# Batch norm's statistics from PSUM, one joined product, an early table load and a changed order of small work in a fused conv/attention kernel

## The chip, the core and the metric

The kernel runs on one core of a Trainium2 chip. A core has TensorE (PE in the profile, with its weight loads as PEld), VectorE (DVE), ScalarE (ACT), GpSimd (POOL) and a SyncE (SP) that here only issues DMAs. All of them run their own list of instructions and meet by semaphores. The metric is the device time of one execution in microseconds (us); the kernel before takes 408.95 us, the median of 3 runs between 408.8 and 410.1.

## What is computed

Six layers follow one another on 8 images of 64 channels by 16x16. The change lies in the first two. The other four are an attention with 8 heads, a mixture of 8 experts, a wavelet attention and a mixture of 16 experts, each behind a layer norm over tokens. Layers one and two of the reference, with what matters:

```python
def _L0_conv_ref(x, Wg, bg, Wt, bt, Wp, bp, Ww, bw, gamma, beta):
    g_x = _maxpool2(_conv1x1(x, Wg, bg))          # pooled values
    theta_x = _conv1x1(x, Wt, bt)                 # queries
    phi_x = _maxpool2(_conv1x1(x, Wp, bp))        # pooled keys
    f_div_C = jax.nn.softmax(jnp.einsum('bni,bim->bnm', theta_x, phi_x), axis=-1)
    y = jnp.einsum('bnm,bmi->bni', f_div_C, g_x)
    w_y = _conv1x1(y, Ww, bw)
    mu = w_y.mean(axis=(0, 2, 3)); var = w_y.var(axis=(0, 2, 3))
    w_y = (w_y - mu) * jax.lax.rsqrt(var + EPS) * gamma + beta
    return w_y + x

def _L1_conv_ref(x, w3, w1, ...):                 # signs of values, signs of weights
    out1 = bn(conv(binary_act(x + b11), bin_weight(w3), pad=1), g1, be1, m1, v1)
    out1 = prelu(x + out1 + b12, a1) + b13
    out2 = bn(conv(binary_act(out1 + b21), bin_weight(w1), pad=0), g2, be2, m2, v2) + out1
    return prelu(out2 + b22, a2) + b23
```

## The kernel before

Each engine's list is written out by hand in one function (`block.tensor`, `block.vector`, `block.scalar` and so on). An engine runs its list in order, so an instruction that waits for a semaphore also holds back everything behind it on that engine. On VectorE the helper `step` makes each small instruction wait for the one before it.

The data of the first two layers lie as 128 partitions (two images by 64 channels) by 1024 columns, worked on in two halves of 512 columns. A half fills one bank of PSUM. The path of layer one is this: TensorE projects the images (L1110); VectorE pools two of the four results and ScalarE adds a bias to the other two, which gives `theta` (L655); TensorE makes the products f (L1118) and a small product for the output weights (L1126). VectorE and ScalarE do the softmax (L1390 to L1405). TensorE meanwhile folds attention weights of layer three (L1132), which needs five loaded weights (`attn_loaded`), and only then transposes the softmax (L1141) and makes w_y (L1148) in banks 4 and 5. ScalarE moves w_y to `wy` with its bias (L678), and VectorE takes the statistics from there (L1416, L1417). Each channel lies on two partitions, so the halves of mean and variance are joined by a product with a constant matrix: first the mean (L1154), then the variance (L1157). ScalarE takes the root of three variances (L682) behind a load of its function table, VectorE makes scale and shift of them, scales both halves and adds the input (L1434, L1435).

Layer two: ScalarE takes the signs (L685), TensorE convolves them in nine products a half (L1169), behind a second fold (L1161). VectorE has ten small instructions for the constants of both norms (L1439 to L1443), a split of folded weights (L1447) and two shifts (L1465) to do before it takes the convolution up (L1456). Then, for each half, VectorE adds (L1456), ScalarE takes the positive part (`positive`, L696), VectorE puts the two together (L1458, L1460), ScalarE takes the second signs (L701) and a shifted copy (L703), TensorE does the second convolution (L1177), and VectorE and ScalarE repeat the step into `x2`. The rest of the kernel (layer norm, attention, experts) follows. The helper `keep_clock` issues products whose result nobody reads; before the change it is called once, far behind.

## Time and profile before

| | us |
|---|---|
| median of 3 runs | 408.95 |
| profiled execution, its own time | 408.8 |
| its span, first to last instruction | 407.0 |
| TensorE busy | 346.5 |
| VectorE busy | 283.3 |
| ScalarE busy | 214.6 |
| GpSimd busy | 174.7 |

The span is what the trace covers; 1.8 us of the execution's own time lie around it. Times in the rows below are us from the span's start. The mean granted clock of TensorE over the span is 0.916 of full speed; it takes two levels only, 1.00 (2.4 GHz) and 0.50 (1.2 GHz). The stretch that the change touches runs from 0 to about 46 us. The idle time in brackets at the end of a row says how long the engine stood still before it and what ended that.

### The profile page before, as it was taken

How to read it: one execution, taken by the hardware profiler on the slowest of the kernel's cores; microseconds unless marked ns; L12 is line 12 of the kernel's file. 1: busy time of each engine (PE TensorE's matmuls, PEld its weight loads, DVE VectorE, ACT ScalarE, POOL GpSimd, SP SyncE). 2: the span in 40 equal slices, each digit the busy share in tenths (PEclk: the TensorE clock that was granted, in tenths of full speed). 3: DMA queues.
4: the chain of work that ended last, by engine and by line, in shares of the span. 5: the costliest groups of instructions: out<-in, count | busy, mean ns of one | idle time of the engine just before them, and what ended most of it. 6: DMA issues, size and time to landing. Idle time of an engine off the chain costs nothing.

```text
span 407.0 us, 6942 instructions
## 1 busy us (share of the span) xinstructions
PE 346.5 (85%) x2177; PEld 244.5 (60%) x2179; DVE 283.3 (70%) x679; ACT 214.6 (53%) x527; POOL 174.7 (43%) x178
## 2 busy tenths in 40 slices
PE   5666368999999999999879799857267999999996
PEld 2552256788788878887567344444065766666662
DVE  2867787788877888787579696687796544555541
ACT  0534357777677767778546544360334534444441
POOL 4020125545455554545410000140110599999984
PEclk9967579999999999999988899988568899999999
DMA  6916000000000000000000794000000866666521
GB/s 184 235 30 209 0 0 2 1 2 3 0 0 0 0 0 0 0 0 2 0 2 3 270 404 159 0 0 2 0 1 13 299 219 208 209 210 217 195 101 52
DMA packets 17002, 32.87 MB, mean 81 GB/s; under 512 B 6032, under 2 KB 9808, under 8 KB 16976
## 3 DMA queue, kind: packets, MB, share of 16 engines
q1 hardware_dynamic: 16976, 32.55, 24.2%
q8 instruction: 13, 0.21, 0.2%
q14 instruction: 13, 0.11, 0.1%
HBM read 31.83 MB, written 0.72 MB: 80 GB/s over the span
## 4 chain that ended last, share of the span: by engine, by line
PE 66%; DVE 18%; ACT 7%; issue 4%; DMA 2%; POOL 0%; SPq 0%; DVEq 0%; ACTq 0%; POOLq 0%
PE ps L1019 15%; PE ps L1027 7%; PE ps L853 7%; PE ps L880 7%; PE ps L864 6%; PE ps L975 4%; ACT va_vb L615 2%; PE ps L967 2%; DVE ln L1501 2%; PE ps L829 2%; DVE negmax L1581 2%; DVE XS L379 2%; PE ps L830 2%; PE ps L906 1%; PE ps L1110 1%
## 5 line engine op out<-in xcount | busy, mean ns | idle before, releaser
L502 POOL TENSOR_TENSOR va_vb<-va_vb,rowinv 128x512 f32<-128x512 f32 x64 | 67.1, 1049 | 72.4 <-DVE rowinv L1588 72.4
L615 ACT ACTIVATE va_vb<-ps,negmax 128x256 f32<-128x256 f32 x128 | 59.4, 471 | 11.9 <-DVE negmax L1581 11.7
L1019 PE MATMUL ps<-XS,w3hl 128*128 128x512 f32 x256 | 64.7, 412 | 0.7 <-ACT gT L586 0.7
L730 ACT ACTIVATE wy<-ps 128x512 f32<-128x512 f32 x64 | 38.2, 598 | 47.3 <-PE ps L1019 47.3
L1019 PEld LDWEIGHTS ps<-XS,w3hl 128*128 128x128 f32 x256 | 49.6, 196 | 17.5 <-issue 4.9
L1581 DVE TENSOR_REDUCE negmax<-ps 128x2 f32<-128x512 f32 x64 | 44.0, 687 | 6.4 <-PE ps L853 4.7
L853 PE MATMUL ps<-keys_gates,xcur 128*128 128x256 f32 x256 | 46.5, 303 | 2.2 <-DVE keys_gates L1573 1.4
L864 PE MATMUL ps<-consts,va_vb 128*128 128x128 f32 x256 | 39.4, 277 | 5.1 <-POOL va_vb L502 3.1
L460 POOL TENSOR_TENSOR xn<-T,lnc 128x512 f32<-128x512 f32 x4 | 4.2, 1041 | 92.0 <-DVE lnc L1509 92.0
L853 PEld LDWEIGHTS ps<-keys_gates,xcur 128*128 128x128 f32 x256 | 34.3, 189 | 14.3 <-issue 11.3
L864 PEld LDWEIGHTS ps<-consts,va_vb 128*128 128x128 f32 x256 | 29.7, 147 | 10.5 <-POOL va_vb L502 4.2
L880 PE MATMUL ps<-pT,vproj 128*64 128x256 f32 x256 | 34.5, 392 | 0.0
L606 ACT ACTIVATE keys_gates<-ps 128x512 fp32r<-128x512 f32 x32 | 19.1, 598 | 25.2 <-PE ps L830 25.2
L615 ACT ACTIVATION_READ_ACCUMULATOR va_vb<-ps,negmax 128x1 f32 x128 | 25.7, 201 | 0.0
L599 DVE COPY pT<-ps 128x512 f32<-128x512 f32 x32 | 21.8, 680 | 1.9 <-PE ps L864 1.9
L1573 DVE TENSOR_TENSOR keys_gates<-ps,keys_gates 128x512 fp32r<-128x512 f32 x32 | 21.8, 682 | 1.6 <-ACT keys_gates L606 1.6
L1674 DVE TENSOR_TENSOR theta_qk<-ps,wy 128x512 f32<-128x512 f32 x16 | 11.1, 691 | 15.3 <-ACT wy L730 15.3
L880 PEld LDWEIGHTS ps<-pT,vproj 128*64 128x64 f32 x256 | 15.6, 136 | 8.9 <-issue 1.4
L597 ACT ACTIVATE pT<-ps 128x512 f32<-128x512 f32 x32 | 19.2, 600 | 0.2 <-PE ps L864 0.2
L1588 DVE RECIPROCAL rowinv<-rowsum 128x2 f32<-128x2 f32 x64 | 10.5, 165 | 11.8 <-ACT va_vb L615 9.6
L967 PE MATMUL ps<-XS,w2hl 128*128 128x512 f32 x64 | 17.9, 430 | 0.5 <-ACT x L722 0.5
L829 PE MATMUL ps<-xcur,AH 128*128 128x256 f32 x64 | 17.1, 288 | 0.1
(321 smaller groups left out, 706.4 us busy)
## 6 DMA issues: line engine op xcount, KB each, us to landing
pT<-gates_row SPq DMA_DIRECT2D x18, 512.0 KB, 4.7
vproj<-gates_row SPq DMA_DIRECT2D x16, 512.0 KB, 5.4
gate_row_keys<-gates_row SPq DMA_DIRECT2D x14, 512.0 KB, 5.2
early<-in_f_in SPq DMA_DIRECT2D x1, 2048.0 KB, 9.1
consts<-in_consts SPq DMA_DIRECT2D x1, 816.0 KB, 5.1
x<-in_x SPq DMA_DIRECT2D x1, 512.0 KB, 3.5
w2raw<-in_f_in SPq DMA_DIRECT2D x1, 512.0 KB, 3.6
out<-in_f_out SPq DMA_DIRECT2D x1, 512.0 KB
```

Source lines behind the costliest of these rows:

```text
L502: gp.tensor_tensor(prob[:, n % 4], prob[:, n % 4], rowinv[:, n % 4, :].unsqueeze(2).broadcast_to([P, U, N]), ALU.mult).then_inc(S("p_scale ...
L599: eng.tensor_copy(dst, src).then_inc(S("pT_odd"), 1)
L615: ins = act.activation(prob[:, n % 4, u, :], ps[:, 1 + n % 2, u * N:(u + 1) * N], ACT.Exp, bias=negmax[:, n % 4, u:u + 1], accum_out=rowsu ...
L730: act.activation(act_out[:, kk % 2, :], ps[:, 2 * (kk % 3), :], ACT.Silu).then_inc(S("f3_act"), 1)
L829: pe.matmul(o, AH[:, head].rearrange("p d c -> p (d c)"), xcur[:, g, :], start=True, stop=False)
L853: mm = pe.matmul(ps[:, 1 + n % 2, u * N:(u + 1) * N], xcur[:, g, u * P:(u + 1) * P], K[:, k % 2, n % 2, :], start=(part == 0), stop=(part ...
L864: mm = pe.transpose(ps[:, 3 + n % 2, su * N + u * P:su * N + (u + 1) * P], prob[:, n % 4, u, su * P:(su + 1) * P], ident)
L880: mm = pe.matmul(ps[h * C:(h + 1) * C, 5, 0:N], vproj[:, g, su, head * C:(head + 1) * C], pT[:, (2 * k + h) % 4, su, :], start=(k % 4 == 0 ...
L967: mm = pe.matmul(ps[:, kk % 4, :], w2hl[:, s, e], XS[:, c * CHUNK:(c + 1) * CHUNK], start=(s == 0), stop=(s == 1))
L1019: mm = pe.matmul(ps[:, 2 * (kk % 3) + w, :], w3hl[:, s, e, w * HID:(w + 1) * HID], XS[:, c * CHUNK:(c + 1) * CHUNK], start=(s == 0), stop= ...
L1027: pe.matmul(ps[half, bank, :], out3[:, e, :], hid[kk % RING], start=False, stop=False, skip_group_check=True).then_inc(S("f3_out_chunk"), 1)
L1581: dve.tensor_reduce(negmax[:, n % 4, :], ps[:, 1 + n % 2, :].rearrange("p (u n) -> p u n", u=U), AX.X, ALU.max, negate=True).then_inc(S("m ...
```

## The change

On ScalarE the table of the exponential is asked for as the first instruction of the kernel. Each half of w_y is counted by VectorE out of PSUM, without the bias, as soon as it is there (`wy_ready`), and ScalarE moves it to `wy` only after that (`wy_counted`). Half means and half variances are joined in one product of two columns; the mean's bias is added afterwards. ScalarE scales the second half (`va_act`) while VectorE scales the first. Sums over weights, two small additions and a sum of squares move to later places on VectorE. In front of the join TensorE runs 5 products of `keep_clock`, and 8 more behind the second fold; they multiply constants of the first convolution. The second signs, shifts and positive parts of layer two are issued in another order on ScalarE.

```diff
--- before.py
+++ after.py
@@ -648,6 +648,7 @@
 
         @block.scalar
         def _(act):
+            act.preload_act_table(ACT.Exp)
             act.wait_ge(S("vec_loaded"), 16)
 
             for p in range(2):
@@ -674,12 +675,15 @@
             act.wait_ge(S("f_transposed"), 1)
             act.activation(probT[:, 0:512], ps[:, 0, :], ACT.Copy).then_inc(S("probT_act"), 1)
             for p in range(2):
-                act.wait_ge(S("wy_ready"), p + 1)
+                act.wait_ge(S("wy_counted"), p + 1)
                 act.activation(wy[:, p * 512:(p + 1) * 512], ps[:, 4 + p, :], ACT.Identity,
                                bias=v_("bw")).then_inc(S("wy_evac"), 1)
 
             act.wait_ge(S("bn_var_ready"), 1)
             act.activation(col[:, 11:14], col[:, 8:11], ACT.Sqrt).then_inc(S("bn_std_ready"), 1)
+            act.wait_ge(S("bn_scale_ready"), 1)
+            act.activation(va[:, 512:1024], wy[:, 512:1024], ACT.Identity, scale=col[:, 28:29],
+                           bias=col[:, 29:30]).then_inc(S("va_act"), 1)
             for p in range(2):
                 act.wait_ge(S("x1_ready"), p + 1)
                 act.activation(sgn[:, 2 * p:2 * p + 2, 1:1 + IMG, 1:1 + IMG],
@@ -695,15 +699,23 @@
                 act.wait_ge(S("prelu_in"), so_far + p + 1)
                 act.activation(vb[:, s], va[:, s], ACT.Relu).then_inc(S("positive_ready"), 1)
 
-            for p in range(2):
-                positive(p, 0)
+            def second_signs(p):
                 act.wait_ge(S("r1_ready"), p + 1)
                 act.activation(sgn2[:, p * 512:(p + 1) * 512], r1[:, p * 512:(p + 1) * 512],
                                ACT.Sign, bias=v_("b21")).then_inc(S("sgn2_ready"), 1)
+
+            def shifted(p):
                 act.activation(va[:, p * 512:(p + 1) * 512], r1[:, p * 512:(p + 1) * 512],
                                ACT.Identity, bias=col[:, 37:38]).then_inc(S("r1_shifted"), 1)
-            for p in range(2):
-                positive(p, 2)
+
+            positive(0, 0)
+            second_signs(0)
+            positive(1, 0)
+            shifted(0)
+            second_signs(1)
+            positive(0, 2)
+            shifted(1)
+            positive(1, 2)
             for half in range(2):
                 act.wait_ge(S("x2_transposed"), half + 1)
                 act.activation(T[:, 8 * half:8 * half + 8, :].rearrange("p t c -> p (t c)"), ps[:, 4 + half, :],
@@ -781,7 +793,7 @@
         def keep_clock(pe, bank, products):
 
             for _ in range(products):
-                pe.matmul(ps[:, bank, :], w3s[:, 0, :], sgn2[:, 0:512], start=True, stop=True)
+                pe.matmul(ps[:, bank, :], w3s[:, 0, :], w3s[:, 4:8, :].rearrange("p k m -> p (k m)"), start=True, stop=True)
 
         def ln_pe(pe, n):
 
@@ -1150,19 +1162,18 @@
                 if j % 2 == 1:
                     mm.then_inc(S("wy_ready"), 1)
 
-            pe.wait_ge(S("bn_mean_half"), 1)
-            pe.matmul(ps[:, 6, 0:1], con("halfavg"), col[:, 0:1], start=True,
-                      stop=True).then_inc(S("bn_mu_done"), 1)
-            pe.wait_ge(S("bn_var_half"), 1)
-            pe.matmul(ps[:, 6, 1:2], con("halfavg"), col[:, 4:5], start=True,
-                      stop=True).then_inc(S("bn_var_done"), 1)
+            pe.wait_ge(S("wsign_ready"), 4)
+            keep_clock(pe, 2, 5)
+            pe.wait_ge(S("bn_halves"), 1)
+            pe.matmul(ps[:, 6, 0:2], con("halfavg"), col[:, 0:2], start=True,
+                      stop=True).then_inc(S("bn_joined"), 1)
 
             for h in range(HEADS):
                 mm = pe.matmul(ps[:, 3, h * C:(h + 1) * C], wvT[:, h, :], wu[:, h, :],
                                start=True, stop=True)
             mm.then_inc(S("folded"), 1)
 
-            pe.wait_ge(S("wsign_ready"), 4)
+            keep_clock(pe, 2, 8)
             for p in range(2):
                 pe.wait_ge(S("sgn_ready"), p + 1)
                 for k in range(9):
@@ -1369,20 +1380,6 @@
             ts(pg[:], pooled[:].unsqueeze(2).broadcast_to([P, J, 2, POOLED]), v_("bpg"), None,
                ALU.add).then_inc(S("pg_ready"), 1)
 
-            dve.wait_ge(S("l1_loaded"), 64)
-            ones = [("w3n", w3n, 9 * C, 20), ("w1n", w1n, C, 21)]
-            for _, w, n, c in ones:
-                step(dve.tensor_reduce(col[:, c:c + 1], w[:], AX.X, ALU.add, apply_absolute_value=True))
-
-            step(ts(col[:, 22:23], col[:, 20:21], 1.0 / (9 * C), None, ALU.mult))
-            step(ts(col[:, 23:24], col[:, 21:22], 1.0 / C, None, ALU.mult))
-            step(ts(col[:, 9:10], v_("v1"), EPS_BN, None, ALU.add))
-            step(ts(col[:, 10:11], v_("v2"), EPS_BN, None, ALU.add))
-
-            dve.wait_ge(S("ns_loaded"), 80)
-            step(dve.tensor_tensor_reduce(nsY[:, 0, :], nsA[:], nsA[:], 1.0, 0.0, ALU.mult, ALU.add, nsc[:, 0:1]))
-            dve.nop().then_inc(S("ns_sq_ready"), 1)
-
             f = ps[:, 5:7, :].rearrange("p a (t c) -> p (a t) c", c=POOLED)
             halves = [slice(8 * half, 8 * half + 8) for half in range(2)]
             for half, q in enumerate(halves):
@@ -1403,6 +1400,13 @@
             step(dve.reciprocal(f_col[:, 2, :], f_col[:, 1, :]))
             for q in halves:
                 tt(f_prob[:, q], f_exp[:, q], wide(f_col[:, 2, q], t=8), ALU.mult).then_inc(S("f_prob_ready"), 1)
+            dve.wait_ge(S("l1_loaded"), 64)
+            ones = [("w3n", w3n, 9 * C, 20), ("w1n", w1n, C, 21)]
+            for _, w, n, c in ones:
+                step(dve.tensor_reduce(col[:, c:c + 1], w[:], AX.X, ALU.add, apply_absolute_value=True))
+
+            step(ts(col[:, 22:23], col[:, 20:21], 1.0 / (9 * C), None, ALU.mult))
+            step(ts(col[:, 23:24], col[:, 21:22], 1.0 / C, None, ALU.mult))
             dve.wait_ge(S("f_transposed"), 2)
             dve.tensor_copy(probT[:, 512:1024], ps[:, 1, :]).then_inc(S("probT_vec"), 1)
 
@@ -1411,27 +1415,38 @@
                 stt(AL[:, :, d, :], ps[:, 7, :].rearrange("p (h c) -> p h c", c=C), 1.0 / math.sqrt(C),
                     AH[:, :, d, :].bitcast(F32), ALU.mult, ALU.subtract).then_inc(S("fold_split"), 1)
 
-            dve.wait_ge(S("wy_evac"), 2)
             for p in range(2):
-                step(dve.bn_stats(bn6[:, p, :], wy[:, p * 512:(p + 1) * 512]))
-            dve.bn_aggr(col[:, 0:2], bn6[:].rearrange("p a s -> p (a s)")).then_inc(S("bn_mean_half"), 1)
-            dve.wait_ge(S("bn_mean_half"), 1)
-            dve.wait_ge(S("bn_mu_done"), 1)
-            step(dve.tensor_copy(col[:, 2:3], ps[:, 6, 0:1]))
-            step(tt(col[:, 3:4], col[:, 0:1], col[:, 2:3], ALU.subtract))
-            stt(col[:, 4:5], col[:, 3:4], col[:, 3:4], col[:, 1:2], ALU.mult, ALU.add).then_inc(S("bn_var_half"), 1)
-            dve.wait_ge(S("bn_var_done"), 1)
-            ts(col[:, 8:9], ps[:, 6, 1:2], EPS_BN, None, ALU.add).then_inc(S("bn_var_ready"), 1)
+                dve.wait_ge(S("wy_ready"), p + 1)
+                dve.bn_stats(bn6[:, p, :], ps[:, 4 + p, :]).then_inc(S("wy_counted"), 1)
+            dve.wait_ge(S("wy_counted"), 2)
+            dve.bn_aggr(col[:, 0:2], bn6[:].rearrange("p a s -> p (a s)")).then_inc(S("bn_halves"), 1)
+            step(ts(col[:, 9:10], v_("v1"), EPS_BN, None, ALU.add))
+            step(ts(col[:, 10:11], v_("v2"), EPS_BN, None, ALU.add))
+
+            dve.wait_ge(S("ns_loaded"), 80)
+            step(dve.tensor_tensor_reduce(nsY[:, 0, :], nsA[:], nsA[:], 1.0, 0.0, ALU.mult, ALU.add, nsc[:, 0:1]))
+            dve.nop().then_inc(S("ns_sq_ready"), 1)
+            dve.wait_ge(S("bn_halves"), 1)
+            dve.wait_ge(S("bn_joined"), 1)
+            step(tt(col[:, 3:4], col[:, 0:1], ps[:, 6, 0:1], ALU.subtract))
+            step(stt(col[:, 4:5], col[:, 3:4], col[:, 3:4], ps[:, 6, 1:2], ALU.mult, ALU.add))
+            ts(col[:, 8:9], col[:, 4:5], EPS_BN, None, ALU.add).then_inc(S("bn_var_ready"), 1)
+            step(tt(col[:, 2:3], ps[:, 6, 0:1], v_("bw"), ALU.add))
             dve.wait_ge(S("bn_std_ready"), 1)
             step(dve.reciprocal(col[:, 24:27], col[:, 11:14]))
 
             step(tt(col[:, 28:29], col[:, 24:25], v_("gamma"), ALU.mult))
             step(tt(col[:, 30:31], col[:, 28:29], col[:, 2:3], ALU.mult))
-            step(tt(col[:, 29:30], v_("beta"), col[:, 30:31], ALU.subtract))
+            tt(col[:, 29:30], v_("beta"), col[:, 30:31], ALU.subtract).then_inc(S("bn_scale_ready"), 1)
+            dve.wait_ge(S("bn_scale_ready"), 1)
+            dve.wait_ge(S("wy_evac"), 2)
             dve.wait_ge(S("l0_loaded"), 32)
             for p in range(2):
                 s = slice(p * 512, (p + 1) * 512)
-                step(ts(va[:, s], wy[:, s], col[:, 28:29], col[:, 29:30], ALU.mult, ALU.add))
+                if p == 0:
+                    step(ts(va[:, s], wy[:, s], col[:, 28:29], col[:, 29:30], ALU.mult, ALU.add))
+                else:
+                    dve.wait_ge(S("va_act"), 1)
                 tt(x1[:, s], va[:, s], x0[:, s], ALU.add).then_inc(S("x1_ready"), 1)
 
             for k, (g_, be, m_, b_) in enumerate((("g1", "be1", "m1", "b12"), ("g2", "be2", "m2", "b22"))):
```

VectorE around the statistics, before: bn is the table of statistics, col the columns of small constants.

```order
L1411 SCALAR_TENSOR_TENSOR AL<-ps,AH 128x8x64 [waits fold_high]
L1411 SCALAR_TENSOR_TENSOR AL<-ps,AH 128x8x64
L1416 BN_STATS bn<-wy 128x6 [waits wy_evac]
L1416 BN_STATS bn<-wy 128x6 [waits dve_step]
L1417 BN_AGGR col<-bn 128x2 [waits dve_step]
L1420 COPY col<-ps 128x1 [waits bn_mu_done,bn_mean_half]
L1421 TENSOR_TENSOR col<-col 128x1 [waits dve_step]
L1422 SCALAR_TENSOR_TENSOR col<-col 128x1 [waits dve_step]
L1424 TENSOR_SCALAR col<-ps 128x1 [waits bn_var_done]
L1426 RECIPROCAL col<-col 128x3 [waits bn_std_ready]
```

The same place on VectorE after the change:

```order
L1415 SCALAR_TENSOR_TENSOR AL<-ps,AH 128x8x64
L1420 BN_STATS bn<-ps 128x6 [waits wy_ready] x2
L1422 BN_AGGR col<-bn 128x2 [waits wy_counted]
L1423 TENSOR_SCALAR col<-vec 128x1
L1424 TENSOR_SCALAR col<-vec 128x1 [waits dve_step]
L1427 ISA nsY,nsc<-nsA 128x64 [waits ns_loaded,dve_step]
L1427 ISA nsc 128x1
L1431 TENSOR_TENSOR col<-col,ps 128x1 [waits dve_step,bn_joined,bn_halves]
L1432 SCALAR_TENSOR_TENSOR col<-col,ps 128x1 [waits dve_step]
L1433 TENSOR_SCALAR col<-col 128x1 [waits dve_step]
L1434 TENSOR_TENSOR col<-ps,vec 128x1
L1436 RECIPROCAL col<-col 128x3 [waits bn_std_ready,dve_step]
```

The statistics read PSUM and wait for the product itself, the second round through TensorE is gone, and four small instructions stand between the sums and the join.

TensorE from w_y to the first convolution, after the change (L796 is `keep_clock`, L1172 the second fold, L1180 the convolution):

```order
L1160 MATMUL ps<-probT_rot,early 128x256
L796 MATMUL ps<-w3s 128x512 [waits wsign_ready]
L796 MATMUL ps<-w3s 128x512 x4
L1168 MATMUL ps<-col,consts 128x2 [waits bn_halves]
L1172 MATMUL ps<-early 128x64 x8
L796 MATMUL ps<-w3s 128x512 x8
L1180 MATMUL ps<-sgn,w3s 128x512 [waits sgn_ready]
```

Before, the list read L1148, L1154, L1157, L1161, L1169: 13 products are new between w_y and the convolution.

ScalarE in layer two, before (r1 is layer two's first result, va_vb the input of the positive part):

```order
L696 ACTIVATE va_vb<-va_vb 128x512
L701 ACTIVATE sgn2<-r1,vec 128x512
L703 ACTIVATE va_vb<-r1,col 128x512
L696 ACTIVATE va_vb<-va_vb 128x512
L701 ACTIVATE sgn2<-r1,vec 128x512
L703 ACTIVATE va_vb<-r1,col 128x512
L696 ACTIVATE va_vb<-va_vb 128x512 x2
```

And after:

```order
L700 ACTIVATE va_vb<-va_vb 128x512 [waits prelu_in]
L704 ACTIVATE sgn2<-r1,vec 128x512 [waits r1_ready]
L700 ACTIVATE va_vb<-va_vb 128x512 [waits prelu_in]
L708 ACTIVATE va_vb<-r1,col 128x512
L704 ACTIVATE sgn2<-r1,vec 128x512 [waits r1_ready]
L700 ACTIVATE va_vb<-va_vb 128x512 [waits prelu_in]
L708 ACTIVATE va_vb<-r1,col 128x512
L700 ACTIVATE va_vb<-va_vb 128x512 [waits prelu_in]
```

Each shifted copy (L708) now stands behind the next positive part (L700) instead of ahead of it.

## Rows read from the trace of the kernel before

**Rows 1.** Chain of waits, 9 to 50 us: start, us, engine, line.

```profile
9.47 0.83 ACT L655
10.30 0.46 issue
...
20.86 2.53 PE ps L1148 x8
...
25.59 0.22 DVE col L1417
...
25.85 0.60 PE ps L1154 x2
...
27.79 3.60 PE ps L1161 x16
31.39 3.97 PE ps L1169 x9
```

**Rows 2.** Busy time by stretch: length, engines' busy us, PEclk, DMA share, GB/s.

```profile
14.50:16.68 2.18, 0.01 (x1) 0.00 (x1) 2.12 (x5) 1.22 (x2) 0.00 (x0) 1.00 0.75 109
16.68:18.60 1.92, 1.92 (x16) 1.86 (x16) 1.85 (x4) 0.00 (x0) 0.00 (x0) 1.00 0.98 277
18.90:22.00 3.10, 3.08 (x11) 2.63 (x12) 1.58 (x3) 1.50 (x3) 2.42 (x2) 0.50 1.24 225
22.10:25.40 3.30, 1.27 (x6) 0.77 (x5) 1.92 (x4) 2.66 (x3) 0.88 (x1) 1.00 0.00 0
25.80:35.60 9.80, 8.98 (x31) 5.98 (x32) 6.86 (x26) 2.14 (x4) 0.00 (x0) 0.50 0.30 96
35.80:42.40 6.60, 2.73 (x13) 1.29 (x12) 4.70 (x8) 4.34 (x7) 0.00 (x0) 1.00 0.52 168
42.90:56.00 13.10, 6.41 (x26) 4.67 (x27) 10.92 (x40) 5.57 (x9) 3.53 (x3) 0.50 0.00 0
```

**Rows 3.** Timeline of TensorE, 10 to 32 us: start, us, instruction, idle before.

```profile
16.68 2.00 PE L1132 MATMUL ps<-early 64*128 64x64 f32 x16 [2.17 <-DMA bu<-in_bu]
18.92 1.94 PE L1141 MATMUL ps<-consts,f_prob 128*128 128x128 f32 x8 [0.24 <-DVE f_prob L1405]
```

**Rows 4.** Instruction groups, 9 to 52 us: reductions from PSUM and from SBUF.

```profile
L1390 DVE TENSOR_REDUCE f_col<-ps 128x8 f32<-128x512 f32 x2 | 1.4, 691 | 0.5 <-PE ps L1118 0.5
...
L1401 DVE TENSOR_REDUCE f_col<-f_both 128x8 f32<-128x512 f32 x2 | 1.3, 680 | 0.0
```

**Rows 5.** Timeline of VectorE, 18 to 46 us.

```profile
21.50 1.28 DVE L1411 SCALAR_TENSOR_TENSOR AL<-ps,AH 128x512 fp32r<-128x512 f32 x2
24.13 1.42 DVE L1416 BATCH_NORM_STATS2 bn<-wy 128x6 f32<-128x512 f32 x2 [1.35 <-ACT wy L678]
...
30.24 0.54 DVE L1434 TENSOR_SCALAR va_vb<-wy,col 128x512 f32<-128x512 f32 x1
30.81 0.69 DVE L1435 TENSOR_TENSOR x<-va_vb,x 128x512 f32<-128x512 f32 x1
31.42 0.15 DVE L1439 TENSOR_TENSOR col<-vec,col 128x1 f32<-128x1 f32 x1
...
35.46 0.75 DVE L1456 SCALAR_TENSOR_TENSOR va_vb<-ps,col,va_vb 128x512 f32<-128x512 f32 x1 [0.62 <-PE ps L1169]
```

**Rows 6.** Timeline of ScalarE, 18 to 50 us.

```profile
24.12 1.28 ACT L682 ACT_TABLE_LOAD   x1
28.02 0.20 ACT L682 ACTIVATE col<-col 128x3 f32<-128x3 f32 x1 [2.62 <-DVE col L1424]
30.36 0.73 ACT L685 ACTIVATE sgn<-x,vec 128x512 bf16<-128x512 f32 x1 [2.13 <-DVE x L1435]
...
38.40 0.71 ACT L703 ACTIVATE va_vb<-r,col 128x512 f32<-128x512 f32 x1
39.01 0.61 ACT L696 ACTIVATE va_vb<-va_vb 128x512 f32<-128x512 f32 x1
...
41.75 0.61 ACT L696 ACTIVATE va_vb<-va_vb 128x512 f32<-128x512 f32 x1
```

## The prediction

> **What bounds the kernel now.** I read the chain of waits first, over the stretch that the change touches, then the granted clock by stretch, then the timelines of the three engines for what each waits on. The chain shows no engine that rules this stretch: it goes from one to the other, a few tenths of a us at a time, and an edit is worth what it takes off that chain until something else is last. Three things show what comes next when a link gets shorter. TensorE's fold L1132 is released at 16.68 us by the landing of a weight, not by any engine [rows 3]. TensorE's clock is low from 18.9 to 22.0, high to 25.4, low again to 35.6, high to 42.4 and low to 56.0; it was still high in the idle 14.5 to 16.7 and in the fold behind it, and fell as the fold ended [rows 2]. And VectorE waits only 0.62 us for the convolution before L1456 [rows 5]: everything that it does from the sums x1 to there is nearly as long as TensorE's convolution at the low clock.
>
> **The change part by part.** Times are of the profiled execution, 408.8 us.
>
> Early table. Before, the load stands between the product and theta: 0.83 us on the chain and 0.46 us behind it [rows 1], 1.29 us together. After, it lies under the wait for the first data. The softmax then comes 1.29 us earlier, but what is late next is the fold: TensorE's transposes L1141 stand behind it, it ends at 16.68 + 2.00 = 18.68 and the transposes started at 18.92 after 0.24 us of waiting for the softmax [rows 3]. So the table can give 0.24 us and no more; the rest is hidden by the weight's DMA, which the change doesn't move. The sums moved behind the softmax are hidden too: VectorE waits there for the transposes, and they end before 20.9 us.
>
> The gap ahead of the fold. TensorE stood idle for 2.17 us before it [rows 3]; with the products ahead of it 1.29 us earlier that is 3.46 us. In the trace of before the clock fell after the shorter gap, once the fold was done [rows 2]; after a longer one I expect the fall to come earlier and the fold to run low. The same number of products at the low clock takes 3.60 us (L1161) [rows 1], 1.60 more. The bounds are 0 and 1.60; I take 1.60. The transposes then start at 16.68 + 3.60 + 0.05 = 20.33, 1.41 us later than before. Their own 1.94 us were already taken at the low clock.
>
> Statistics from PSUM. Before, from the start of the transposes (18.92) to the end of the sums (25.59 + 0.22 = 25.81) [rows 1] it took 6.89 us. After, the sums start when VectorE is through with L1411, which ended at 21.50 + 1.28 = 22.78, 3.86 after the transposes' start; two sums of 1.42 us together and the last of 0.22 [rows 5, 1] with 0.05 between make 5.55. The evacuation's 0.69 us leaves the path, and so does waiting for both halves. The sums from PSUM are not in the trace; a reduction from PSUM takes 691 ns and one from SBUF 680 [rows 4], so from -0.05 to +0.1 us for both, and I take 0. w_y must be there in time: L1148 starts as the transposes end and takes 2.53 us, of which about 1.2 at the low and 1.3 at the high clock [rows 1, 2]; ending 4.47 after the transposes' start it is ready for the second sum at 4.57. Wholly low it would be 1.2 + 2 x 1.3 = 3.8 us, 1.2 us late: that is this term's upper bound. I take 5.55, so the sums end at 25.88, 0.07 later than before: the fold has eaten what the statistics saved.
>
> Five products before the join. Nine take 3.97 us at the low clock [rows 1], 0.44 each, and half of that, 0.22, at the high one. Beside the sums (1.4 us from w_y's end to the last sum) lie 1.1 us of them at the high clock, which cost nothing; at the low one 2.2 us, which cost 0.8.
>
> Join. Before, from the sums to the root 25.81 to 28.02, 2.21 us [rows 1, 6]. After, one product (0.60) [rows 1] and three small instructions of about 0.2 each with their waits: 1.35 us, which is 27.23. The four small instructions put in front of them take about 0.7 us beside the join's 0.65. But ScalarE's table for the root comes after the second evacuation, and that now waits for the second sum: 20.33 + 5.28 = 25.61, plus 0.69 + 0.05, plus 1.28 [rows 6] is 27.63. Before, the table was in at 25.40 and the root waited 2.62 us for its input [rows 6]; now the table is the last to come. Root at 27.65 instead of 28.02: 0.37 gained.
>
> ScalarE scales a half. From the root to the end of x1 it took 28.02 to 31.50, 3.48 us; VectorE's second L1434 of 0.54 goes [rows 5] and its gap of 0.03, while ScalarE does it in some 0.73 us [rows 6] beside VectorE's first half of 1.2. That leaves x1 done at 30.56, 0.94 ahead of before.
>
> Convolution. What is late next is VectorE. Its ten small instructions, split and shifts took from 31.42 to 35.46 - 0.62 = 34.84, 3.42 us [rows 5]; overlapping by 0.08 as before they now end at 30.48 + 3.42 = 33.90. TensorE: join done at 26.55, fold 2.0 and eight products 1.8 at the high clock make 30.3; the signs come at 30.36 - 0.37 + 0.73 = 30.72 [rows 6]; nine products at the high clock are ready at 32.8, before VectorE. So L1456 starts at 33.92 instead of 35.46, 1.54 gained, and the 1.2 us by which a fast convolution beats VectorE are hidden. At the low clock it would be ready at 30.72 + 3.97 = 34.69, which costs 0.77.
>
> Order in layer two. The positive part L696 of the second half starts at 39.01, behind the shifted copy begun at 38.40; its input was ready by then [rows 6]. The same happens again before 41.75. Putting the copies behind takes 0.6 off twice, 1.2 us; the copies still end before VectorE needs them. Bounds 1.0 and 1.2.
>
> Sum: 1.54 + 1.2 = 2.7 us, 408.8 - 2.7 = 406.1. The median of before is 0.15 above the profiled execution, so 406.2. From x2 on the kernel is unchanged and moves forward as a whole.
>
> A rule weighed. The trace has the table's load at 1.28 us, and theta started at 10.76, right at its end (9.47 + 1.28) [rows 1, 6]. The Trainium skill (ScalarE: Activation LUTs, "What ACT_TABLE_LOAD costs") adds a drain of about 1.38 us to every switch, 2.66 in all. By the trace the sum stands at 406.2; by the page's drain behind the root's table it would be 407.6, a rival below.
>
> **The rivals.**
> 1. The fold stays high, as before: the transposes start at 18.70, everything behind comes 1.6 us earlier, 404.6. For it: before, the clock was still high through the fold, to 18.6 [rows 2]. Against it: the longer gap.
> 2. The root's table is followed by a pause of ScalarE, put at one more load's length, 1.28 us [rows 6]: 407.5. Against it: theta's start. For it: the only other load of this stretch, the root's, was hidden before, and now it is the last to come. With it go a convolution at the low clock (407.0) and a start of the attention, now 2.7 us earlier, in the low stretch that ended at 56.0 [rows 2].
> 3. The eight products run low: join 26.55, fold 3.6, products 3.5, convolution 3.97 is ready at 37.6, 2.2 later than L1456 before; less the order's 1.2 it is 410.0, no difference.
> 4. The other side: the clock stays low from w_y to the convolution. w_y is 1.2 late (26.1), five products 2.2 (28.3), join 0.65, fold 3.6, eight products 3.5, convolution 3.97: L1456 at 40.0, 4.5 late, less 1.2, 412.3. It decides as soon as the fold and the eight products need more than the 4.2 us from join to signs. For it: the second fold did not raise the clock in 25.8 to 35.6 although TensorE was busy 8.98 us of 9.80 [rows 2]. Against it: the clock was up again right behind that stretch, with nothing but the convolution before it, and the new products are of its kind. The Trainium skill (TensorE: Matmul & The Clock Gate, "What's actually happening") has activity release the throttle, which would make the products pay; no run here shows it for them.
>
> **How the numbers follow.** A change within 0.3% (1.2 us) can't be told from none. Forecast 406.2: 0.46, its own range 405.4 to 407.0. Rival 1: 0.22. Rival 2 and its like, 407.0 to 407.7: 0.10. Rival 3: 0.14. Rival 4: 0.08. Faster is the first three, 0.78; same 0.14; slower 0.08. The range runs from just under rival 1, 404.2, to 408.8, into the cases of no difference.
>
> **What would show it.** Right: no table load before theta; the fold at 16.7 to about 20.3 with the clock at 0.5; the sums released by L1411, not by a copy; the root right behind its table load; L1456 with no wait for TensorE; no copy ahead of L700 in layer two. Wrong: a fold that ends at 18.7 (rival 1), a gap between table and root (2), signs ready long before the convolution starts (3 and 4).

## The result and the profile after

| | before | after |
|---|---|---|
| median, us | 410.06 (20 runs, 408.45 to 411.85) | 408.18 (20 runs, 405.09 to 412.35) |
| profiled execution, own time, us | 408.8 | 409.88 |
| its span, us | 407.0 | 408.1 |
| mean granted clock | 0.916 | 0.912 |

The ratio after to before is 0.9949 (0.9932 to 0.9967), 2.1 us faster (1.35 to 2.8). The forecast was faster by 2.7, 406.2. The three runs of before that it started from had a median of 408.95; twenty have 410.06, and that accounts for 1.1 of the 2.0 us by which the absolute figure is off. The profiled execution of after is one of its longer ones, 1.7 us above its median, so two questions have to be kept apart: what the changed stretch does, and what this execution lost elsewhere. The profiled execution of before is one of its shorter ones, 1.3 us under the median of twenty.

The chain of waits of after over the stretch that changed (start, us, engine, line):

```profile
10.55 6.07 DMA bu<-in_bu
16.66 3.67 PE ps L1144 x16
20.33 1.90 PE ps L1153 x8
22.23 3.69 PE ps L1160 x8
25.94 0.71 DVE bn L1420
26.68 0.69 ACT wy L679
27.38 1.28 ACT L683
28.68 0.21 ACT col L683
...
30.36 1.29 DVE x L1450 x2
...
33.50 0.63 DVE GL L1462
34.13 0.86 DVE va_vb L1480 x2
35.02 0.76 DVE va_vb L1471
```

The line numbers have moved: the fold L1132 is now L1144, w_y L1148 is L1160, the sums L1416 are L1420, the root L682 is L683, the first multiply-add behind the convolution L1456 is L1471. Against [rows 1] five things are to be seen. The softmax is gone from the chain; a DMA stands in its place and goes straight into the fold. The fold takes 3.67 us instead of 2.00 [rows 3], and the transposes start at 20.33. w_y takes 3.69, and the second sum comes right behind it. The root's table load stands on the chain, and the root follows at its end (27.38 + 1.28 = 28.66; 28.68). And TensorE's second fold and convolution, 7.57 us of the chain before [rows 1], no longer stand on it: from the root to L1471 all is VectorE.

The granted clock of after by stretch (columns as in [rows 2], the engines in the order PE, PEld, DVE, ACT, POOL):

```profile
14.50:16.66 2.16, 0.00 (x1) 0.01 (x1) 2.10 (x5) 0.97 (x2) 0.00 (x0) 0.90 0.75 100
16.66:20.33 3.67, 3.67 (x17) 3.55 (x18) 2.98 (x8) 0.00 (x0) 1.04 (x1) 0.50 1.13 274
20.33:25.90 5.57, 5.57 (x17) 4.32 (x18) 2.58 (x4) 2.33 (x4) 2.35 (x1) 0.50 0.36 56
26.00:40.00 14.00, 9.80 (x50) 5.03 (x48) 11.75 (x37) 7.84 (x12) 0.00 (x0) 0.98 0.46 152
211.00:219.00 8.00, 8.00 (x80) 6.87 (x79) 5.28 (x27) 2.85 (x6) 0.00 (x0) 0.50 0.01 3
```

The same late stretch of before, in code that the change doesn't touch:

```profile
211.00:219.00 8.00, 7.30 (x89) 5.80 (x89) 7.12 (x33) 4.24 (x8) 0.00 (x0) 0.85 0.00 1
```

Before, the clock was high through the fold, low over the transposes and high again over the second part of w_y [rows 2]. In after it falls in the idle time ahead of the fold and stays at 1.2 GHz (0.50) until 25.9, over the fold, the transposes and all of w_y; from 26 it is up, and the second fold and the convolution run at 2.4 GHz. In the last row the whole gate computation, unchanged, is at the low clock, where before had it mostly high. That is why this execution is longer than before's although its first layer norm is earlier. Its root (L570) starts at 48.80 instead of 50.36, and the second layer norm's root at 208.73 instead of 210.00; but the copies of the gates (L586) start at 222.18 instead of 221.21. So 1.56 us are gained in the changed stretch, 0.3 given back up to the second norm, and 2.2 in the gates. From the first norm's root to the end of the span it is 356.6 us in before and 359.3 in after, in the same code and with the same mean granted clock there, 0.93: what differs is where the low stretches fall.

### The profile page after: what moved, and what is told of

Its sections match the earlier page's. It is cut to its first block, busy times and chain, and to the rows that moved or that the text cites. A ratio compares the mean times of both kernels' runs of the same rounds, so it can differ in the third digit from the quotient of the medians.

```text
span 408.1 us, 6967 instructions
## 1 busy us (share of the span) xinstructions
PE 351.4 (86%) x2190; PEld 247.5 (61%) x2190; DVE 283.1 (69%) x678; ACT 216.2 (53%) x528; POOL 174.8 (43%) x178
## 4 chain that ended last, share of the span: by engine, by line
PE 56%; DVE 18%; issue 10%; ACT 7%; POOL 3%; DMA 3%; SPq 2%; POOLq 0%; DVEq 0%; ACTq 0%
PE ps L1031 15%; PE ps L1039 7%; PE ps L865 5%; PE ps L892 5%; PE ps L987 4%; PE ps L876 4%; POOL va_vb L502 2%; SPq L385 2%; ACT va_vb L615 2%; PE ps L979 2%; DVE ln L1516 2%; DVE negmax L1596 2%; DMA bu<-in_bu 1%; PE ps L803 1%; DVE XS L379 1%
## 5 line engine op out<-in xcount | busy, mean ns | idle before, releaser
L865 PE MATMUL ps<-keys_gates,xcur 128*128 128x256 f32 x256 | 47.4, 308 | 1.8 <-DVE keys_gates L1588 1.8
L803 PE MATMUL ps<-consts,xn 128*64 128x128 f32 x64 | 10.5, 334 | 9.6 <-DVE xn L1534 9.6
```

Source lines behind the costliest of these rows:

```text
L865: mm = pe.matmul(ps[:, 1 + n % 2, u * N:(u + 1) * N], xcur[:, g, u * P:(u + 1) * P], K[:, k % 2, n % 2, :], start=(part == 0), stop=(part ...
```

## The experiments

Each kernel is after or before with the edits named. None leaves out a part of the computation; added `keep_clock` products are work that nobody reads. Ratios are to the kernel before on the same chip, whose median was 410.4 to 410.5 each time. A gain in us is taken from the ratio where nothing else is said.

### The early table and the fold

**late_table**: after, with the exponential's table asked for where it was before.

```diff
-            act.preload_act_table(ACT.Exp)
             act.wait_ge(S("vec_loaded"), 16)
```

> The changed kernel, with the exponential's table loaded where it was before, at the first use. Theory (the early table gains nothing, because the fold still waits for its weights at 16.6 us, and it lengthens TensorE's idle time ahead of the fold so that the fold runs at the low clock, 3.67 us instead of 2.00): faster than the changed kernel by about 1 us, so some 3.1 us under the kernel before; the fold again near 2.0 us in most executions. Rival (the 1.29 us of the table are on the path): slower than the changed kernel by 1.3 us, some 0.8 us under the kernel before.

Measured: 406.08, ratio 0.9913 (0.9881 to 0.9946), 3.6 us faster than before, and faster than after by 1.5 (by the ratios, whose intervals just overlap) to 2.1 us (by the medians). TensorE's timeline (start, us, instruction, idle before), the fold of after first and then late_table:

```profile
16.66 3.67 PE L1144 MATMUL ps<-early 64*128 64x64 f32 x16 [3.00 <-DMA bu<-in_bu]
...
16.83 2.00 PE L1143 MATMUL ps<-early 64*128 64x64 f32 x16 [1.98 <-DMA bu<-in_bu]
19.26 1.94 PE L1152 MATMUL ps<-consts,f_prob 128*128 128x128 f32 x8 [0.44 <-DVE f_prob L1401]
21.13 2.68 PE L1159 MATMUL ps<-probT_rot,early 128*128 128x256 f32 x8
```

With 1.98 us of gap instead of 3.00 the fold is back at 2.00 us, and the transposes wait only 0.44 for the later softmax. To take this part of the change away gains 1.5 us with about as much uncertainty, which is at the edge of the noise.

**early_table_only**: before, with nothing but the early table.

```diff
+            act.preload_act_table(ACT.Exp)
             act.wait_ge(S("vec_loaded"), 16)
```

> The kernel before with nothing but the early load of the exponential's table. Theory (the softmax then waits for nothing but the fold, which ends at 16.7 us plus its own length, and the longer idle time ahead of it lets TensorE's clock fall sooner): the fold takes 3.6 us instead of 2.0 in most executions and everything behind it is 1 us later; 0.5 to 1.5 us slower than the kernel before. Rival (the load was on the path): 1.3 us faster.

Measured: 411.26, ratio 1.0027 (1.0006 to 1.0048), 1.1 us slower (0.25 to 2.0). Its fold:

```profile
16.85 3.52 PE L1133 MATMUL ps<-early 64*128 64x64 f32 x16 [2.47 <-DMA bu<-in_bu]
20.30 1.97 PE L1142 MATMUL ps<-consts,f_prob 128*128 128x128 f32 x8
```

The softmax does come earlier, the fold doesn't wait for it and runs low, and the transposes stand at 20.30, where the forecast put them (20.33). So this edit costs more than it gives: clear of the noise where it is added to before, at the edge of it where it is taken out of after. All ten traces without products in that gap agree: with the late table the fold took 2.00 us in before, late_table, stats_only and order_only and 2.25 in order_again; with the early one 3.67 in after, 3.52 here, 3.42 in old_order, 2.92 in no_fill and 2.49 in split_later. The means are 2.05 and 3.20, 1.15 us apart.

**fill_before_fold**: after, with twelve unread products in the gap ahead of the fold.

```diff
+            pe.wait_ge(S("wsign_ready"), 4)
+            keep_clock(pe, 2, 12)
             pe.wait_ge(S("attn_loaded"), 80)
```

> The changed kernel with 12 more unread products on TensorE in its idle time ahead of the first fold, 13.7 to 16.6 us. Theory (the fold's clock is what the early table lost): the fold takes 2.0 us and ends at about 18.7, transposes and w_y are 1.6 us earlier or more, and with them all that follows: about 2 us faster than the changed kernel, some 4 us under the kernel before. Rival (what ends last there is not the fold, or the products hold it back): within 0.5 us of the changed kernel or slower, at most 2.1 us under the kernel before.

Measured: 405.4, ratio 0.9885 (0.9854 to 0.9916), 4.7 us faster than before; its interval lies wholly under after's (0.9932 to 0.9967). TensorE:

```profile
13.36 2.75 PE L796 MATMUL ps<-w3s 128*128 128x512 bf16 x12
16.79 2.00 PE L1146 MATMUL ps<-early 64*128 64x64 f32 x16 [0.68 <-DMA bu<-in_bu]
18.71 1.29 PE L1155 MATMUL ps<-consts,f_prob 128*128 128x128 f32 x8
20.54 3.75 PE L1162 MATMUL ps<-probT_rot,early 128*128 128x256 f32 x8 [0.54 <-ACT probT_rot L676]
```

With the idle time cut to 0.68 us the fold is at 2.00 us again, this time with the table early, and even the transposes begin high (1.29). It is what TensorE does in the gap that makes the fold slow, not the table as such. w_y is still at the low clock here: that fall has not been cured, only the one ahead of it. The first layer norm's root starts at 47.41, 1.4 us ahead of after's; the rest of the 2.6 us by which the ratios differ is not placed.

### The order of layer two on ScalarE

**order_only** and **order_again** (the same kernel, measured twice): before, with after's order.

```diff
-            for p in range(2):
-                positive(p, 0)
...
+            positive(0, 0)
+            second_signs(0)
+            positive(1, 0)
+            shifted(0)
```

> The kernel before, with nothing but the new order of second signs, positive parts and shifted copies on ScalarE. Theory: 1.2 us under the kernel before (twice 0.6), and from the first L1456 to the end of x2 some 8.7 us instead of 9.9. Rival (VectorE has other work in that time, the copies are only moved): within 0.3 us of the kernel before.

> The kernel before with only the new order on ScalarE once more, for twice the executions. Theory: the trace showed it 0.7 us shorter from the first L1464 to the first layer norm (the second half of the convolution, at the low clock, waits there), so the kernel is 0.7 us under the kernel before, and the first result was short of executions. Rival (what is gained there is given back behind it): within 0.3 us of the kernel before once more.

Measured: 410.38, ratio 1.0004 (0.9984 to 1.0024), and 410.54, ratio 0.9996 (0.9976 to 1.0017). No gain in either; together 0.0 ± 0.6 us. **old_order** is the reverse, after with before's order:

> The changed kernel with the old order of second signs, shifted copies and positive parts on ScalarE, all else as changed. Theory (the new order is worth twice 0.6 us once the convolution runs at the high clock and VectorE never waits for its second half): about 1.1 us slower than the changed kernel, 1.0 us under the kernel before instead of 2.1, and from the first L1471 to the end of x2 some 9.9 us instead of 8.8. Rival (as the kernel before with only the new order, which gained nothing): no slower than the changed kernel, 2.1 us under the kernel before.

Measured: 408.44, ratio 0.995 (0.993 to 0.997): not to be told from after, though the two intervals together leave room for some 1.1 us either way. By the medians no gain of the order is to be seen; the forecast had 1.2 us for it. The traces don't say the same. ScalarE in after:

```profile
37.32 0.72 ACT L704 ACTIVATE sgn<-r,vec 128x512 bf16<-128x512 f32 x1 [0.89 <-DVE r L1475]
37.99 0.63 ACT L700 ACTIVATE va_vb<-va_vb 128x512 f32<-128x512 f32 x1
38.52 0.71 ACT L708 ACTIVATE va_vb<-r,col 128x512 f32<-128x512 f32 x1
```

and in old_order:

```profile
36.29 0.72 ACT L705 ACTIVATE sgn<-r,vec 128x512 bf16<-128x512 f32 x1 [0.89 <-DVE r L1467]
36.92 0.70 ACT L707 ACTIVATE va_vb<-r,col 128x512 f32<-128x512 f32 x1
37.53 0.61 ACT L700 ACTIVATE va_vb<-va_vb 128x512 f32<-128x512 f32 x1
```

In after the positive part follows the signs at once, 0.67 after their start; in old_order it stands behind the copy, 1.24 after it, as in [rows 6]. From the first multiply-add to the first layer norm's root every trace with the new order takes 13.8 us and every one with the old 14.9 (before 35.46 to 50.36, after 35.02 to 48.80), save order_only with 14.2. So the order gives 1.1 us where it acts (0.7 in order_only). What becomes of it outside that stretch differs: in the traces of order_only and order_again the first multiply-add came 0.6 and 0.3 us later than in before, in unchanged code, and more was lost behind. In order_only a part of that is to be seen on the chain, at the first scores of the attention:

```profile
57.94 1.22 PE ps L861 x4
59.16 0.21 PE ps L837
```

in order_again the same work at the other clock:

```profile
57.24 0.74 PE ps L861 x4
57.98 0.12 PE ps L837
```

0.5 us in one group, for products that came at another moment of the clock. Between executions such losses change place, and one trace of a kernel doesn't give their mean. **best_old_order** asked again where the clock is better kept (best, below, with before's order):

> The kernel of the run before this one with the old order on ScalarE. Theory: from the first multiply-add of the convolution to the first layer norm's root 14.9 us instead of 13.8, and 1.1 us slower in all. Rival (given back behind): no slower.

Measured: 405.83, ratio 0.9882 (0.9852 to 0.9912), against 404.5 and 0.984 (0.9804 to 0.9875) with the new order: 1.3 us by the medians, 1.7 by the ratios, about the size of theory, but the intervals overlap. What the order is worth in the whole kernel stays open between 0 and 1.7 us; added to before by itself, none of it reaches the end.

### Statistics, join, half and fills

**stats_only**: before, with the sums from PSUM, the single join, ScalarE's half and the moved small instructions; no early table, no fills, old order.

```diff
-            act.preload_act_table(ACT.Exp)
...
-            keep_clock(pe, 2, 5)
...
-            keep_clock(pe, 2, 8)
```

(The diff is against after, beside the order.)

> The kernel before with the statistics from PSUM, the one join and ScalarE's half, and the small instructions in their new places; no early table, no unread products, the old order. Theory: the sums end 1.3 us earlier, the root starts 1.8 us earlier behind its table, x1 is done 2.4 us earlier and L1469 or what stands for it starts 2.2 us earlier, after waiting up to 0.8 us for a convolution at the low clock: 2.2 us under the kernel before. Rival (the parts need each other: without the unread products the fold and the convolution, both low, take the gain back): under 1 us below the kernel before.

Measured: 409.76, ratio 0.9972 (0.9952 to 0.9993), 1.15 us faster (0.3 to 2.0). The interval leaves theory's 2.2 out and doesn't settle the rival's "under 1". The transposes on TensorE, then VectorE:

```profile
19.61 1.63 PE L1144 MATMUL ps<-consts,f_prob 128*128 128x128 f32 x8 [0.69 <-DVE f_prob L1391]
...
23.19 0.69 DVE L1409 BATCH_NORM_STATS2 bn<-ps 128x6 f32<-128x512 f32 x1
24.26 0.70 DVE L1409 BATCH_NORM_STATS2 bn<-ps 128x6 f32<-128x512 f32 x1 [0.38 <-PE ps L1151]
...
34.18 0.75 DVE L1460 SCALAR_TENSOR_TENSOR va_vb<-ps,col,va_vb 128x512 f32<-128x512 f32 x1 [0.88 <-PE ps L1169]
```

The multiply-add starts at 34.18, 1.28 ahead of [rows 5], after 0.88 us of waiting for a convolution that is partly at the low clock. Without it VectorE would have been ready at 33.3. Its steps come later than theory had them, because the transposes start 0.69 us later than in [rows 3]. Counted from their start, the sums end after 5.59 us (6.89 in before), the root starts after 7.38 (9.10) and x1 is done after 10.36 (12.58): 1.3, 1.7 and 2.2 us saved, where theory had 1.3, 1.8 and 2.4. So the statistics do what they should up to there, and part of it is lost to the later transposes and to the convolution.

**no_fill**: after without both of its new groups of unread products.

> The changed kernel without the 5 and the 8 unread products. Theory (they keep the clock high for the first convolution, which is then hidden behind VectorE): the second fold and the convolution run at the low clock in most executions, L1471 waits for TensorE by up to 0.8 us, and the kernel is some 0.5 us slower than the changed one, about 1.5 us under the kernel before. Rival (they only take TensorE's time, since VectorE ends last there anyway): no slower than the changed kernel, 2.1 us or more under the kernel before.

Measured: 407.93, ratio 0.9955 (0.9933 to 0.9977): not to be told from after. In its trace the wait of stats_only is back:

```profile
34.77 0.75 DVE L1469 SCALAR_TENSOR_TENSOR va_vb<-ps,col,va_vb 128x512 f32<-128x512 f32 x1 [0.98 <-PE ps L1178]
```

In after there is no such wait. The fills do what they are for, and it is worth 0.98 us at that place in this trace; in the median it doesn't show, and the two intervals leave room for some 1.1 us either way. Inconclusive.

Two kernels settle more when they are put side by side: late_table is stats_only with the new order and the 13 products, and nothing else. Their ratios, each to before on its own chip, are 0.9913 (0.9881 to 0.9946) and 0.9972 (0.9952 to 0.9993): the intervals don't meet, and order and products together are worth 2.4 us. VectorE in late_table:

```profile
32.95 0.75 DVE L1470 SCALAR_TENSOR_TENSOR va_vb<-ps,col,va_vb 128x512 f32<-128x512 f32 x1
```

Nothing is waited for here, and the step starts 3.38 us behind the end of x1, where stats_only needs 4.21; from there to the first layer norm's root it is 13.78 instead of 14.89. The root is at 46.73 instead of 49.07, 2.34 us earlier: 1.11 by the order, 0.83 by the products that spare the wait, 0.40 ahead of x1's end. How the 2.4 us of the medians divide between the two is not shown.

### Taking the forecast's next bound away

**split_later**: VectorE's split of the second fold (0.69 us, [rows 5] has it in the 3.42) moves into the first layer norm, where VectorE waits for ScalarE; the fold and the join change banks so that it may wait, and TensorE's own wait for the split moves from ahead of the second convolution to ahead of the attention.

```diff
-            dve.wait_ge(S("fold_high"), 3)
-            tt(GL[:], ps[:, 3, :], GH[:].bitcast(F32), ALU.subtract).then_inc(S("fold_split"), 1)
...
+                    if n == 0 and q == 8:
+                        dve.wait_ge(S("fold_high"), 3)
+                        tt(GL[:], ps[:, 6, :], GH[:].bitcast(F32), ALU.subtract).then_inc(S("fold_split"), 1)
```

> The changed kernel with VectorE's split of the second fold (0.69 us, L1462) moved from ahead of L1471 to the layer norm, into the 0.8 us in which VectorE waits there for the second half; the second fold and the join change banks for it. Theory (VectorE's queue from x1 to L1471 is what ends last once the convolution is fast): L1471 starts 0.7 us earlier and the layer norm is not longer: 0.7 us faster than the changed kernel, 2.8 us under the kernel before. Rival (the convolution is the bound): VectorE waits for it instead, no gain, 2.1 us under the kernel before.

Measured: 407.29, ratio 0.9911 (0.9881 to 0.9942), 3.6 us faster than before. That goes the way of theory, but its interval overlaps after's. In the trace the multiply-add is released by the instruction before it on its own engine, not by TensorE:

```profile
32.41 0.88 DVE L1478 TENSOR_SCALAR va_vb<-x,col 128x512 f32<-128x512 f32 x2
33.53 0.75 DVE L1469 SCALAR_TENSOR_TENSOR va_vb<-ps,col,va_vb 128x512 f32<-128x512 f32 x1 [0.24 <-DVE va_vb L1478]
```

It starts 2.97 us behind the end of x1 (30.56), where after needs 3.37: 0.40 of the 0.7 us that theory had, with the same 2.97 or 2.98 in best and best_old_order below. From there to the first layer norm's root it is 13.77 us, as in after, so the norm is not longer.

**fill_norms**: fill_before_fold, and unread products ahead of the first two layer norms, where TensorE idles (10 and 5).

```diff
+            keep_clock(pe, 2, 10)
             ln_pe(pe, 0)
...
+            keep_clock(pe, 4, 5)
             ln_pe(pe, 1)
```

> The changed kernel with 12 unread products ahead of the first fold, 10 ahead of the first layer norm's transposes and 5 ahead of the second's. Theory (the spread between executions, and part of the time, is the clock being low where the norms' products and the start of the attention and of the experts come): about 1 us faster than with the 12 alone, some 6 us under the kernel before, and the slowest executions come nearer to the fastest. Rival (the products there are hidden or hold the norms back): no faster than with the 12 alone, 5 us or less under the kernel before.

Measured: 405.88, ratio 0.9862 (0.9831 to 0.9892), 5.7 us faster. Its interval overlaps that of fill_before_fold: whether the products at the norms pay is undecided. The slowest executions don't come nearer to the fastest: 403.0 to 410.96, against 404.13 to 407.05 with the 12 alone, six executions each.

**best**: fill_norms and split_later together.

> The changed kernel with the split of the second fold in the layer norm, 12 unread products ahead of the first fold, 10 ahead of the first layer norm's transposes and 5 ahead of the second's. Theory: 0.7 us faster than the same without the later split, 6 us or more under the kernel before. Rival (with the products in place VectorE is no longer the bound there): as without the later split, 5 to 5.7 us under the kernel before.

Measured: 404.5 (402.49 to 405.38), ratio 0.984 (0.9804 to 0.9875), 6.6 us faster than before (5.1 to 8.0); its interval lies wholly under after's. Theory's 6 and the rival's 5 to 5.7 both lie in it, so what the later split adds in the median is undecided. TensorE and then VectorE of its trace:

```profile
16.74 2.10 PE L1146 MATMUL ps<-early 64*128 64x64 f32 x16 [0.81 <-DMA bu<-in_bu]
...
20.66 2.58 PE L1162 MATMUL ps<-probT_rot,early 128*128 128x256 f32 x8
...
29.21 4.22 PE L1182 MATMUL ps<-sgn,w3s 128*128 128x512 bf16 x18 [0.79 <-ACT sgn L689]
```

```profile
31.96 0.75 DVE L1473 SCALAR_TENSOR_TENSOR va_vb<-ps,col,va_vb 128x512 f32<-128x512 f32 x1 [0.24 <-DVE va_vb L1482]
```

The fold is at 2.10, w_y at 2.58, and the multiply-add at 31.96, 3.1 us ahead of after's and 3.5 ahead of before's.

## Why the prediction was right, and where it was not

The direction and the size of the gain held: 2.1 us in the medians (1.35 to 2.8) against 2.7 forecast, and a first layer norm 1.56 us earlier in the trace. Its making held up to the convolution; two steps did not, the clock over w_y and the order's way to the end. By its steps:

- **Early table and fold: right.** The 0.24 us was the ceiling, the longer gap cost more. The fold took 3.67 us where 3.60 was taken, and the transposes were forecast at 20.33 and stand there. Rival 1 (a fold that stays high) fell; fill_before_fold and late_table give its condition back and come out 4.7 and 3.6 us under before, where the rival had 4.35 (408.95 less 404.6). The 1.60 us taken was the upper end of its bounds; over the five traces with the early table the fold is 1.15 us longer on the mean, and early_table_only is 1.1 slower.
- **Statistics from PSUM: right in kind, at the bound in this execution.** A sum from PSUM takes 0.70 us where 0.71 from SBUF was taken [rows 5]. The wait is for w_y: the forecast let the clock fall earlier, but carried over before's w_y, half low, 2.53 us; wholly low was named as the bound, 1.2 us late. It came out wholly low:

```profile
24.24 0.70 DVE L1420 BATCH_NORM_STATS2 bn<-ps 128x6 f32<-128x512 f32 x1
25.94 0.70 DVE L1420 BATCH_NORM_STATS2 bn<-ps 128x6 f32<-128x512 f32 x1 [1.01 <-PE ps L1160]
```

  The sums end at 26.89 instead of 25.88, and everything up to the multiply-add is 1.0 to 1.1 late: root 28.68 for 27.65, x1 31.65 for 30.56, L1471 35.02 for 33.92. This is the mis-sized term of the sum: 3.75 us here, and more than 2.53 in each of the five traces with the early table and no products ahead of the fold (2.79 to 3.75). What holds the sum up is the fold, which in four of the five is shorter than the 3.60 taken. Fold and w_y together were forecast at 6.13 us and took 6.24 to 6.33 in early_table_only, old_order, no_fill and split_later, but 7.42 in after. So x1 is done at 30.62, 30.45 and 30.56 in old_order, no_fill and split_later, within 0.11 of the forecast's 30.56, and in old_order, whose program is after's up to L1471, that step stands at 33.99. The path was right; how the low stretch would divide between fold and w_y was not foreseen, and that the two deviations cancel in the sum is luck. The clock over w_y is not a property of the kernel but of the execution.
- **Join and root: right.** The root's table is last to come, and the root starts at its end, 1.30 us behind its start. Rival 2 (a pause behind the load) fell. The drain that the Trainium skill (ScalarE: Activation LUTs, "What ACT_TABLE_LOAD costs") adds to a switch does not appear between this load and its root: of the 1.30 us from 27.38 to 28.68 the load itself takes 1.28, which leaves no room for a drain of 1.38.
- **ScalarE's half: right.** From the root to the end of x1, 28.68 to 31.65, 2.97 us; forecast 2.91, before 3.48.
- **VectorE becomes the bound: right.** L1471 starts with no wait, 3.37 us after x1 (forecast 3.36), and the convolution at the high clock, 4.22 us for both halves from 31.87 on, has its first half done by about 34.0 (31.87 and half of 4.22). Rivals 3 and 4 fell: the eight products ran at 0.24 us each (1.90 for 8) and the clock was up from 26.
- **Order of layer two: right where it acts, not shown for the whole.** 1.2 us were forecast, and 1.1 are there up to the first layer norm's root. But order_only and order_again gain none in total, and old_order shows no loss. The step that failed is "moves forward as a whole": what lies behind is not shifted unchanged, since the clock's low stretches fall elsewhere in it. The same code behind the first norm's root took from 356.6 us (before) to 361.6 (old_order) in the ten traces where it is unchanged. Where the 1.1 goes on the average isn't settled; best_old_order, and late_table beside stats_only, suggest that it stays where the clock is kept up.

In the trace of after the low w_y takes 1.1 us off the forecast's gain, and the gates take more than the 1.56 that are left; in the medians 2.1 us remain, with an interval that holds the 2.7. Step by step, by the ratios, before to stats_only is 1.15 us gained, the order and the products add 2.4 (late_table), and the early table takes some 1.5 back (after). Without the 1.41 us by which it let the fold delay the transposes, the forecast's gain is 4.15, where late_table measured 3.6 (2.2 to 4.9). That the total came this near, with one term too small and one not to be found alone, is in part luck.

## What to carry to other kernels

An instruction moved earlier gains only up to the next thing that it waits for, and if that is a DMA, the time gained turns into idle time of the engine behind it; ask what that engine's clock does in a longer gap before you count the move as free. A stretch bound by a chain of short waits is improved by its last link only: find with the timeline of each engine which would be next (here VectorE, with a split that could wait; 0.40 us of its 0.69 came off), and change that too. Where an engine's clock moves between executions, one trace shows a mechanism and not a mean: test a term of a us by a kernel with that term alone, in both directions, and two terms that may need each other by a kernel with both: here the order alone gained nothing on before, and order and products together 2.4 us.

## What the runs showed of the hardware

- The same instructions, identical up to that point of the program, met the low clock at different places: w_y took 3.75 us in after, 2.90 in old_order; the fold 3.67 and 3.42. After's times spread over 405.09 to 412.35. The Trainium skill (TensorE: Matmul & The Clock Gate, "What's actually happening") says that the monitor's window runs freely and is not reset by a kernel, so the place of a change differs from run to run; these traces agree in that the place differs, and of the window itself they show nothing.
- The length of the idle time in the records doesn't order the folds among themselves: 2.17 us of it and a fold of 2.00 in before, 2.14 and 3.42 in old_order, 3.87 and 2.49 in split_later, 2.35 and 2.25 in order_again. When the table was asked for tells more than the gap of one execution.
- Products of 512 columns in bfloat16 filled into a gap kept the fold high in all four kernels that had them there: 2.00, 2.00, 2.10 and 2.26 us.
- In seven of the ten kernels with the new statistics the exponential of the gates (L580), whose code is unchanged, starts 7.56 to 7.58 us behind the second norm's root, where before and the three kernels with only the order or only the early table have 7.28 to 7.30: in before 210.00 to 217.28, in best 206.14 to 213.71, in order_again 209.38 to 216.68. In the other three, after, stats_only and split_later, it is 8.52 to 9.52. Some 0.3 us of what the change gains is so given back in unchanged code; why was not tried and stays open.
